# Attention and gate stage of a two-stage transformer block: scores summed on one engine, x added by transposes, softmax reciprocal and residual copy on ScalarE, new instruction orders

## The reference

```
n  = layernorm(x);  q = rotary(n Wq), k = rotary(n Wk)  # 16 half-heads of 16
v  = n Wv                                               # 8 heads of 32
# within ONE token, over its own heads n and m:
s_c[n,m] = q[n,c,:] . k[m,c,:] / 2,  c = 0,1            # 2 x 8 x 8 scores
p_c = softmax_m(s_c);  a = (p_0 - lam * p_1) v
a  = a / rms(a) * ln_w + ln_b, scaled;  x1 = x + a Wo
# feed-forward: 8 experts, top 2 of softmax(layernorm(x1) w_gate), capacity 1024
out = x1 + sum over the token's two experts of weight * (silu(h_a) * h_g) W2
```

## Time and profile before

| | |
|---|---|
| median of 3 runs (lowest, highest) | 734.85 us (734.85, 737.51) |
| profiled execution: its own time / its span | 735.65 us / 733.7 us |
| mean granted TensorE clock | 0.962 |
| TensorE busy | 666.2 us (91%) |
| VectorE busy | 549.8 us (75%) |
| POOL busy | 511.4 us (70%) |
| ScalarE busy | 445.5 us (61%) |
| first stage, until the last indirect DMA to the table | 0 to 492.7 us |
| second stage, from its first transpose | 497.9 us to the end |

### The profile page before, as it was taken

The page is one execution under the profiler, slowest core; times in us unless marked ns, Lnnn a source line. Parts: engine busy times, 40 slices in busy tenths (PEclk is TensorE's granted clock), DMA queues, the critical chain, the costliest instruction groups (busy, mean ns, idle before and its releaser), DMA issues.

```text
span 733.7 us, 13227 instructions
## 1 busy us (share of the span) xinstructions
PE 666.2 (91%) x3896; PEld 538.8 (73%) x3896; DVE 549.8 (75%) x1386; ACT 445.5 (61%) x1402; POOL 511.4 (70%) x294
## 2 busy tenths in 40 slices
PE   5889999999999999999999998407999999999991
PEld 2567787787777778778777876306888988988881
DVE  2998999999999999999999998503454554654540
ACT  1546777777777777777777775703554555555440
POOL 3445548888888888888888796571666675675635
PEclk9989999999999999999999999856999999999996
DMA  7980012222221222211101100102547556556334
GB/s 219 341 274 1 30 43 76 74 97 73 74 95 67 93 77 74 95 52 46 59 30 30 31 29 8 52 2 88 124 88 145 130 118 119 141 131 90 58 35 53
DMA packets 57822, 63.47 MB, mean 87 GB/s; under 512 B 7433, under 2 KB 53614, under 8 KB 57760
## 3 DMA queue, kind: packets, MB, share of 16 engines
q1 hardware_dynamic: 42400, 45.66, 19.3%
q0 software_dynamic: 15360, 17.08, 13.5%
HBM read 27.57 MB, written 43.78 MB: 97 GB/s over the span
## 4 chain that ended last, share of the span: by engine, by line
PE 82%; DVE 8%; issue 4%; POOL 3%; DMA 2%; ACT 1%; SPq 0%; POOLq 0%; DVEq 0%; ACTq 0%
PE bank_a L736 14%; PE bank_qk L701 13%; PE bank_qk L818 9%; PE bank_wo L750 7%; PE bank_v L709 7%; PE bank_wo L829 5%; PE bank_v L818 5%; PE bank_a L818 4%; PE bank_a L829 4%; PE bank_a L742 4%; PE bank_s L717 3%; DVE s_part L932 2%; PE bank_t L692 2%; DVE qk_dve L926 2%; POOL slot_table L405 1%
## 5 line engine op out<-in xcount | busy, mean ns | idle before, releaser
L225 POOL TENSOR_TENSOR v_prod<-w_att,v_sb 128x2048 f32<-128x2048 f32 x62 | 232.3, 3747 | 83.1 <-DVE w_att L963 47.4
L405 POOL DMA_INDIRECT slot_table<-rows,g_slot x128 | 130.1, 1016 | 39.5 <-issue 31.7
L442 POOL DMA_INDIRECT out_dram<-y_sb,e_tok x64 | 99.7, 1557 | 65.0 <-ACT y_sb L625 50.5
L736 PE MATMUL bank_a<-ident,v_prod 128*128 128x128 f32 x1024 | 124.2, 275 | 5.3 <-DVE aT_n L970 5.3
L736 PEld LDWEIGHTS bank_a<-ident,v_prod 128*128 128x128 f32 x1024 | 117.3, 142 | 13.2 <-issue 5.5
L701 PE MATMUL bank_qk<-wqkv,xT 128*128 128x512 f32 x256 | 120.5, 593 | 1.4 <-DVE wqkv L873 1.4
L926 DVE TENSOR_TENSOR qk_dve<-bank_qk,k_sb 128x1536 f32<-128x1536 f32 x64 | 111.9, 1748 | 0.0
L932 DVE TENSOR_REDUCE s_part<-qk_dve 128x128 f32<-128x1536 f32 x64 | 111.8, 1747 | 0.0
L750 PEld LDWEIGHTS bank_wo<-wo_aug,aT_n 128*128 128x128 f32 x256 | 48.4, 191 | 35.2 <-issue 24.4
L750 PE MATMUL bank_wo<-wo_aug,aT_n 128*128 128x265 f32 x256 | 68.7, 391 | 2.7 <-DVE x_ring L975 2.6
L701 PEld LDWEIGHTS bank_qk<-wqkv,xT 128*128 128x128 f32 x256 | 43.7, 190 | 37.4 <-issue 30.6
(11 more groups left out here) (169 smaller groups left out, 1466.2 us busy)
## 6 DMA issues: line engine op xcount, KB each, us to landing
slot_table<-fill SPq DMA_DIRECT2D x8, 1056.0 KB, 13.0
xe<-slot_table SPq DMA_DIRECT2D x16, 528.0 KB, 3.7
x_ring<-in_L_attn_x_dram SPq DMA_DIRECT2D x16, 512.0 KB, 3.5
out_dram<-x_ring SPq DMA_DIRECT2D x16, 512.0 KB, 3.1
w<-in_L_ffn_c_fc_dram SPq DMA_DIRECT2D x8, 768.0 KB, 5.2
w<-in_L_ffn_c_proj_dram SPq DMA_DIRECT2D x8, 384.0 KB, 5.9
slot_table<-rows,g_slot POOLq DMA_INDIRECT x128, 2.5
out_dram<-fill SPq DMA_DIRECT2D x1, 1024.0 KB, 13.4
```

Source lines behind the costliest of these rows:

```text
L225: eng.tensor_tensor(v_prod[b][:, :, :].rearrange("p m (n e) -> p m n e", n=H), w_att[b][:, :, :].rearrange("p n m -> p m n").unsqueeze(3). ...
L405: pool.indirect_dma_start(out=table, out_offset=bass.IndirectOffsetOnAxis(ap=g_slot[gb][:, j, k:k + 1], axis=0), in_=rows[:, r, :], in_off ...
L442: pool.indirect_dma_start(out=out, out_offset=bass.IndirectOffsetOnAxis(ap=e_tok[n % 2][:, k:k + 1], axis=0), in_=y_sb[n % 2][:, k, :], in ...
L736: last = nc.tensor.matmul(bank_a[b][:, k * P:(k + 1) * P], v_prod[b][:, m, k * P:(k + 1) * P], ident[:, :], is_transpose=True, start=(m == ...
```

## The change

What it does, by engine:

- All 16 depths are multiplied in one VectorE instruction of 2048 elements and summed in one reduction that writes the scores into PSUM (`scores`, two buffers in bank_s). `sum_scores`, `sum_scores_part`, `scores_to_tokens` on TensorE and `copy_sT` on ScalarE go.
- `attention_added` on VectorE goes. `out_project` starts bank_wo with the bias, adds x by transposing xT back (two transposes that accumulate), then adds the projection; xT therefore has 10 buffers. `copy_x1` on ScalarE takes x1 out of PSUM.
- The reciprocal of the softmax sum becomes ln and exp on ScalarE, with layernorm's factor for v added in the exponent (`half_ln`), so `copy_v` needs no scale. ln_w is multiplied into Wo once (`wo_s`), and `scale_a` is a plain product.
- Gate: a new addition `g_both`; row_tokens and row_experts move to ScalarE; g_hot, g_max, g_rec, g_count, g_slotf and the expert numbers lie in bank_s. Groups are 14 of four tiles and 4 of two at the end. The x ring has 20 tiles, the row ring 12, the slot buffer 8.
- The lags and the order of each engine are new; the scatter lags by 11 tiles and stands ahead of `head_products`.

```diff
+GROUPS = (4,) * 14 + (2,) * 4
 def score_products(t):
-    qk_pe  (4 depths, 512 elements)  and  qk_dve (12 depths, 1536 elements)
+    nc.vector.tensor_tensor(qk_prod[b] ... 2 * D, q4, k4, ALU.mult).then_inc(qk_multiplied, 1)
+def score_sum(t):
+    past(dve, ssub_ready, t, 2)
+    nc.vector.tensor_reduce(scores[b] ..., qk_prod[b] ..., AX_X, ALU.add).then_inc(scores_ready, 1)
 def out_project(t):
+    nc.tensor.matmul(bank_wo, ones, bias_parts, start=True, stop=False)
+    for k in range(2): nc.tensor.matmul(bank_wo[k], xT[t % XT][:, k, :], ident, is_transpose=True)
     past(pe, an_ready, t)
+    for k in range(2): nc.tensor.matmul(bank_wo, aT_n[b][k], wo_s[:, k, :], stop=(k == 1))
+def prob_reciprocal(t):                       # ScalarE
+    nc.scalar.activation(p_ln, p_sum, ACT.Ln)
+    nc.scalar.activation(p_rec, p_ln, ACT.Exp, bias=half_ln[s], scale=-1.0)
+def copy_x1(t):                               # ScalarE
+    nc.scalar.activation(x_ring[E + NEXP], bank_wo[E + NEXP], ACT.Identity, bias=aux_x[NEXP])
+    nc.scalar.copy(x_ring[0:E + NEXP], bank_wo[0:E + NEXP]).then_inc(x1_ready, 1)
...
 # order on VectorE, tile part (gate operations between these are left out)
+score_subtract(i-1) prob_difference(i-2) score_products(i) prob_sum(i-1) score_sum(i)
+prob_normalise(i-1) score_max(i) scale_a(i-3)
 # order on ScalarE
+prob_reciprocal(i-4) copy_k(i-2) rms_a(i-6) copy_x1(i-7) squares2(i-7) squares1(i-3) copy_v(i-3)
+roots(i-3) copy_xT(i) exp_scores(i-3) square_a(i-5) normalise2(i-9) copy_aux(i-2) log_a(i-5)
 # order on TensorE
+project_qk(i-2) sum_heads(i-6) positions project_v(i-3) mean_squares(i-6) out_project(i-7) transpose_x(i)
 # order on POOL
+scatter(i-11) head_products(i)
```

More of the change, by code:

```diff
@@ L23 @@
 GROUP = 4
[L24 to L28, removed]
-AUX = NEXP + 1
+RING = 20
+ROWS = 12
+XT = 10
+SLOT_BUFS = 8
+AUX = NEXP + 1
+GROUPS = (4,) * 14 + (2,) * 4
+LAST = [sum(GROUPS[:g + 1]) - 1 for g in range(len(GROUPS))]
+FIRST = [LAST[g] + 1 - n for g, n in enumerate(GROUPS)]
+LN2_LATER = 4
+SLOTS_BEFORE_X = 11
 XW = E + AUX + 1
@@ L114, in build_block @@
             stat_ln = one("stat_ln", [P, RING, 2])
-            rstd = one("rstd", [P, RING, 2])
             rstd_sq = one("rstd_sq", [P, RING])
+            half_ln = one("half_ln", [P, RING])
+            rstd = one("rstd", [P, RING])
             neg_mr = one("neg_mr", [P, RING])
+            aux_x = one("aux_x", [P, RING, AUX])
             sq_junk = one("sq_junk", [P, 2, E])
-            xT = pair("xT", [P, 2, P])
+            xT = [one(f"xT{b}", [P, 2, P]) for b in range(XT)]
             k_sb, v_sb = pair("k_sb", [P, E]), pair("v_sb", [P, E])
[L121 to L124, removed]
+            qk_prod = pair("qk_prod", [P, H * H * 2 * D])
             s_max = pair("s_max", [P, 2 * H])
@@ L148, in build_block @@
             g_sel = pair("g_sel", [P, GROUP, 2, NEXP])
-            g_slotf, g_slot = pair("g_slotf", [P, GROUP, 2]), pair("g_slot", [P, GROUP, 2], I32)
+            g_slot = [one(f"g_slot{b}", [P, GROUP, 2], I32) for b in range(SLOT_BUFS)]
         xe = [sb(f"xe{b}", [P, CB, ROW]) for b in two]
@@ L229, in head_products, with row_free, run_tiles, live @@
                 ALU.mult).then_inc(multiplied, 1)
[L231 to L237, removed]
-            for i in range(NT + LAG_MAX):
[L240 to L252, removed]
+        def row_free(eng, t):
+            if t >= ROWS:
+                eng.wait_ge(scattered[t % ROWS], (t // ROWS) * 32)
+        def run_tiles(step):
+            for i in range(NT + LAG_MAX):
+                step(i)
+        def live(t):
+            return 0 <= t < NT
+        def closes(t):
+            return t in LAST
+        def group_of(t):
+            return LAST.index(t)
         CHUNKS = NEXP * NCH
@@ L581, in step @@
-                if live(i, 6):
-                    log_a(i - 6, u % 2)
-                g, gb = group_step(i, u, q, 12)
-                if g is not None:
-                    exp_gate(g, gb)
-                if live(i, 5):
-                    square_a(i - 5, (u - 5) % 2)
-            run_tiles(act, step)
+                if i == 5:
+                    scale_wo()
+                if live(i - 6):
+                    rms_a(i - 6)
+                if live(i - 7):
+                    copy_x1(i - 7)
@@ L591, in weights_high @@
+                if live(i - 3):
+                    exp_scores(i - 3)
+                if live(i - 5):
+                    square_a(i - 5)
+                if live(i - 9):
+                    normalise2(i - 9)
+                if live(i - 2):
+                    copy_aux(i - 2)
+                if live(i - 5):
+                    log_a(i - 5)
+            run_tiles(step)
             def weights_high(e, b):
@@ L787, in step @@
                     transpose_wo()
[L788 removed]
+                if i == 4:
                     fold_gate()
[L790 removed]
+                if i == 5:
                     bias_row()
[L792 to L798 removed]
@@ L800, in _ @@
-            run_tiles(pe, step)
-            pe.wait_ge(slot8_ready, NG)
+                if live(i - 6):
+                    sum_heads(i - 6)
+                if closes(i - 11):
+                    positions(group_of(i - 11))
+                if live(i - 3):
+                    project_v(i - 3)
+                if live(i - 6):
+                    mean_squares(i - 6)
+                if live(i - 7):
+                    out_project(i - 7)
+                if i == 0:
+                    qk_means()
```

696 lines of the change are left out of this document (363 added, 333 removed).

## The result

| | before | after |
|---|---|---|
| median (lowest, highest) | 735.01 us (734.85, 737.51), 4 runs | 700.49 us (699.26, 701.0), 4 runs |
| profiled execution: time / span | 735.65 / 733.7 | 699.26 / 697.4 |
| mean granted TensorE clock | 0.962 | 0.966 |
| start, until tile 7's product on VectorE | 61.20 | 59.74 |
| tile 7's product to tile 63's | 379.85 (6.78 for a tile) | 356.30 (6.362) |

Ratio of the times 0.952 [0.9496, 0.9544]: faster by 34.5 us. In the profiled executions the span is 36.3 us shorter, and the stretches account for all of it: 1.46 at the start, 23.55 in the steady stretch, 11.32 at the end of the first stage.

What follows compares the result with a forecast made beforehand. TensorE was taken to set 6.78 us a tile, with 48.0 us at the first stage's end a bound of its own. 735.65 - 18.5 (steady stretch) - 10.9 (end) = 706.2, forecast 706 us; 8 in 10 within 693 to 722.

Steps and rivals of the forecast that it cites:

- TensorE, 6.34: Steady stretch: transposes removed and added make TensorE net 0.44 us less per tile, from 6.78 to 6.34.
- VectorE, 6.37: Steady stretch: 5.72 us for the tile's own instructions plus 0.65 for gate work; bounds 6.28 and 6.44.
- rival 4: The change doesn't do what it says, for instance a slower reduction into PSUM on VectorE: 725 us; chance 0.05.
- POOL, 6.34: Steady stretch: POOL's time for one product and two scatters stays unchanged at 6.34 us per tile.
- ScalarE, 5.9: Steady stretch: ScalarE goes from 5.03 to 5.9 us per tile with the added instructions; upper end 6.47.
- rivals 1 and 3: ScalarE becomes the bound, 720 us, chance 0.12; ScalarE's in-order queue stalls every engine, 760 us, chance 0.05.
- Steady pace 6.45: Steady stretch: 6.45 us per tile (6.28 to 6.65), gaining 18.5; floor 6.37 exactly, with a wait-free end, had chance 0.03.
- The start, 0: Until tile 7's product (61.20 us before): no change, bounds 4 us either way.
- The end, 10.9: End of first stage: 48.0 us behind POOL's last product become 37.1, with 26 scatters left; gain 10.9, bounds 2 to 14.7.
- Rival 2: End of first stage: the last tile's chain, not the scatter count, decides; gain 2 instead of 10.9, 715 us; chance 0.15.
- Gate operands in PSUM, nothing: VectorE's gate work: one PSUM input costs nothing (185 against 184 ns); the skill page's fixed costs would add 7 us.
- The long scatters: End of first stage: both VectorE products meet a POOL scatter and lengthen it, 2 x 1.9 us more.

Runs made afterwards that it cites:

- e8: Changed kernel with 16 groups of four tiles instead of 14 of four and 4 of two: 702.45 us, ratio 0.9572.
- e11: Changed kernel with the gate's operands (g_hot, g_max, g_rec, g_count, g_slotf, expert numbers) back in SBUF: 720.44 us, ratio 0.9808.
- e1: Changed kernel with one extra pair of 128x128 transposes per tile on TensorE: 712.15 us, ratio 0.969.
- e2: Changed kernel with one extra short reduction per tile on VectorE: 712.24 us, ratio 0.9689.
- e7: Changed kernel without the two transposes that add x on TensorE, and with 1920 instead of 2048 elements in VectorE's product and reduction: 689.89 us, ratio 0.9397.
- e4: Changed kernel with one extra 128x128 copy per tile on ScalarE: 700.79 us, ratio 0.9534.
- e9: Changed kernel in which VectorE takes the last three of POOL's products instead of the last two: 704.3 us, ratio 0.9586.
- e10: Changed kernel in which VectorE takes the last four of POOL's products instead of the last two: 704.97 us, ratio 0.9604.
- e12: Changed kernel with the last three products on VectorE, and 13 groups of four and 6 of two: 702.95 us, ratio 0.9568.
- e3: Changed kernel with an extra 128x256 memset on POOL ahead of each product of tiles 0 to 61: 706.03 us, ratio 0.9611.

## Why the prediction was right, and where it was not

Forecast 706 (693 to 722), measured 700.49: the case was the forecast's, a faster steady stretch and a shorter end. The step that was off is the pace of the steady stretch. Of the change's parts only the groups of two (e8) and the gate operands (e11) were taken back one by one; what the new orders, the longer lags and the 10 buffers of xT are worth by themselves was not tried. By the forecast's steps:

- **TensorE, 6.34.** Right. The four tiles of a group take 25.37, 6.34 each, and e1 shows that TensorE binds.
- **VectorE, 6.37.** Right: 5.72 for the tile's own instructions as forecast, with 2 x 2.20 for the score work instead of 2 x 2.19, and 0.62 for the gate instead of 0.65. e2 shows that it binds as well. That the reduction into PSUM might be slower (rival 4) is refuted by 2282 ns.
- **POOL, 6.34.** Mis-sized: it is 6.22 (e7). The distance in the earlier trace rows, 6.34, was not POOL at its shortest: the scatter at 155.44 between the two products took 1.09, where the others of that stretch take 0.98 to 1.00. It did no harm, as POOL's floor lies under the other two, but it was the third engine of the argument "three within 0.5% of each other".
- **ScalarE, 5.9.** 319.54 / 56 = 5.71: the estimate was 0.2 high, and rivals 1 and 3, in which its order or its load stops the others, did not come. e4 shows 0.2 more (319.54 to 330.49 busy) to be free. The squares wait 0.36 in a tile (23.1 / 64) where they waited 1.12; as argued, the additions used that.
- **Steady pace 6.45.** This is the term that was mis-sized: a margin of about 0.08 over the floor, put there for engines that are late for another in turn and for the tight spot before mean_squares. Measured 6.362, the floor itself; 56 x 0.09 = 5 of the 6.9 us by which the profiled execution (699.26) lies under the sum (706.2). The start's 1.5 and the end's 0.4 are the rest. Two engines with the same floor cost each other nothing here: the steady gain was 23.55, which the text had only in its 0.03 case.
- **The start, 0.** Measured 1.46 shorter, inside the bounds of 4. No experiment was made on it, and this mark lies anywhere from 59.47 to 61.06 in e8, e9, e10 and e12, whose edits change nothing before tile 7; so whether the start gained at all stays open.
- **The end, 10.9.** Measured 11.6 from the end of POOL's last product (48.0 to 36.4), 11.3 from tile 63's product. The terms hold: 33.3 for 26 scatters, 2.8 for two long scatters instead of 3.8. What was not seen is what the stretch hangs on. Before the change, tile 52's slots were ready at 457.34, 16.3 us after tile 63's product; after the change, at 422.31, 6.3 us after it. That is 10.0 of the 11.3 us. That the rest hangs on these slots is shown by e9 and e10; that they come earlier because the new order works on them with less lag is read from the code and wasn't tried by itself. Rival 2 named the chain of the last tile. That chain didn't decide: its slots were ready at 443.90, and its group's scatters began at 451.57. What rival 2 had right is that slots decide, those of an earlier group; its outcome was wrong, because these came earlier too.
- **Gate operands in PSUM, nothing.** Wrong as a value of the edit, though the sum came out. The text asked only what PSUM costs, and that is next to nothing, as it said (175 to 178 ns for g_sub and g_over, against 184 and 185 in the earlier trace rows; against e11, at most 10 ns more for one instruction, the reciprocal's 176 against 166). It did not ask what the operands in SBUF would cost in the new order: 20 us. The sum was right only because it assumed without saying so that gate work keeps its price when it is moved. In e11 it doesn't.
- **The long scatters.** Taken from the row at 448.75, against the inference of the Trainium skill, page "SBUF — State Buffer", section on who interferes with whom, that a two-input VectorE operation doesn't hold up the making of descriptors. The runs contradict it again: two scatters took 2.57 and 2.21 against 0.97. Each scatter that began beside such a product of VectorE, in the kernel before, in the changed one and in every experiment, ended 0.84 to 0.86 us after that product.

## What to carry to other kernels

Add up each engine's instructions by the distance between starts and forecast the largest sum; in this kernel, whose buffers are two deep and more, two equal engines needed no margin (6.37 and 6.34 gave 6.362). That the buffers are the reason was not tried. Busy shares don't tell who binds, since time in which an instruction is held counts as busy (VectorE in e7): one small instruction more on each engine in turn does, and so does relieving two engines together when each alone brings nothing. When VectorE's work is moved, mark each instruction with two SBUF inputs and see whether it now starts during a long GpSimd product: with 32 elements it took 1.54 us here, and 0.18 with one operand in PSUM.

## What was not expected of the hardware

- A VectorE subtraction of 32 elements a partition took 1539 ns on average beside POOL's product and 175 with one input in PSUM (e11).
- In VectorE's full queue an instruction costs less than its span: the 2048-element product 2.20 of 2.28 us, a 128-element one 0.20 of 0.28.
- Indirect DMAs on POOL go out 1.28 us apart, 0.97 and a pause of 0.30, also without any other work on POOL, for all the last 20.
- An indirect DMA that begins beside VectorE's 128x2048 product with two SBUF inputs takes 2.08 to 2.88 us in all traces and ends 0.84 to 0.86 after that product. In e3, 34 of them begin beside VectorE's 2048-element product with one input in PSUM and take 0.97 to 0.98.
